# A recurrence whose output gate is summed last, and a quantised feed-forward layer unrolled over the sequences

## The reference, cut to what matters

```python
def step(carry, xg_t):
    h, c = carry
    g = xg_t + h @ W_hh.T
    i, f, gg, o = jnp.split(g, 4, axis=-1)
    c = jax.nn.sigmoid(f) * c + jax.nn.sigmoid(i) * jnp.tanh(gg)
    h = jax.nn.sigmoid(o) * jnp.tanh(c)
    return ((h, c), h)
```

```python
def act_quant_fake(x):
    scale = 127.0 / jnp.clip(jnp.max(jnp.abs(x), axis=-1, keepdims=True), 1e-05)
    return jnp.clip(jnp.round(x * scale), -128.0, 127.0) / scale
# h = layernorm(x) * g1 + b1;  u = gelu(bitlinear(h, w1, b1))
# n = layernorm(u) * g2 + b2;  y = bitlinear(n, w2, b2);  x = layernorm(x + y)
```

## Time and profile before

| what | value |
| --- | --- |
| median of three runs | 2242.31 us (2241.83 to 2244.61) |
| the profiled execution | 2243.14 us, of which the span of instructions is 2241.3 us |
| PE busy | 1638.2 us, 73% of the span |
| DVE busy | 1314.2 us, 59% |
| ACT busy | 912.4 us, 41% |
| POOL busy | 567.8 us, 25% |
| chain that ended last | PE 54%, issue 21%, DVE 8%, ACT 6%, POOL 5% |

### The profile page before, as it was taken

How to read it: one execution, slowest core, us unless ns; L and a number is a source line. 1 busy time by engine, 2 the same in 40 slices (tenths; PEclk the granted TensorE clock), 3 DMA queues, 4 the chain that set the end, 5 groups by cost and what they waited for, 6 DMA issues and landing times.

```text
span 2241.3 us, 44676 instructions
## 1 busy us (share of the span) xinstructions
PE 1638.2 (73%) x14699; PEld 1050.1 (47%) x14699; DVE 1314.2 (59%) x4045; ACT 912.4 (41%) x2545; POOL 567.8 (25%) x937
## 2 busy tenths in 40 slices
PE   4545389667775557898768822159989999996997
PEld 3333255445443335554435511135657777774443
DVE  2333566556666765613756767757756666663776
ACT  2222344456641113443435433223336665653443
POOL 2321422211212223300222233422224334342010
PEclk9999999789986768998989955579989999997999
DMA  5000000000000000000020000000000000000000
GB/s 192 1 1 1 1 1 0 0 1 0 0 0 0 0 0 0 1 1 1 0 82 15 1 1 0 0 1 1 0 1 1 0 0 0 0 1 0 0 0 19
DMA packets 2930, 18.30 MB, mean 8 GB/s; under 512 B 1050, under 2 KB 1178, under 8 KB 1562
## 3 DMA queue, kind: packets, MB, share of 16 engines
q1 hardware_dynamic: 2842, 17.17, 2.0%
HBM read 16.06 MB, written 1.05 MB: 8 GB/s over the span
## 4 chain that ended last, share of the span: by engine, by line
PE 54%; issue 21%; DVE 8%; ACT 6%; POOL 5%; DVEq 3%; POOLq 3%; DMA 0%; ACTq 0%; SPq 0%
PE ps L2876 5%; PE ps L922 3%; PE ps L936 3%; PE ps L2441 3%; PE ps L2451 3%; PE ps L2465 3%; PE ps L2420 3%; PE ps L2427 3%; PE ps L991 2%; PE ps L1502 2%; POOL arena L362 2%; PE ps L2285 2%; PE ps L344 2%; PE ps L901 2%; PE ps L556 1%
## 5 line engine op out<-in xcount | busy, mean ns | idle before, releaser
L362 POOL TENSOR_TENSOR arena<-arena,C 128x1 f32<-128x1 f32 (+1 forms) x240 | 137.5, 575 | 728.1 <-DVE arena L373 415.5
L1081 DVE TENSOR_REDUCE arena<-ps 128x4 f32<-128x512 f32 x256 | 164.0, 685 | 88.3 <-PE ps L932 49.2
L457 POOL TENSOR_TENSOR arena<-arena,C 128x512 f32<-128x512 f32 x96 | 100.0, 1042 | 364.0 <-ACT arena L658 127.2
L2378 POOL TENSOR_TENSOR arena<-arena 128x512 f32<-128x512 f32 x128 | 132.9, 1044 | 233.5 <-DVE arena L2666 232.9
L1049 ACT ACTIVATE arena<-ps 128x512 f32<-128x512 f32 x256 | 132.2, 602 | 89.3 <-PE ps L948 89.3
L1502 PE MATMUL ps<-hid,WA 128*20 128x16 f32 x1024 | 57.8, 197 | 104.9 <-DVE hid L1547 104.9
L2876 PE MATMUL ps<-WA,arena 128*128 128x512 f32 x256 | 133.5, 603 | 0.4 <-ACT arena L2900 0.4
L2575 ACT ACTIVATE arena<-ps,arena 128x256 f32<-128x256 f32 x256 | 120.1, 479 | 11.9 <-issue 8.1
L2584 ACT COPY arena<-ps 128x512 f32<-128x512 f32 x128 | 69.1, 589 | 121.4 <-PE ps L2451 121.4
L2658 DVE TENSOR_REDUCE arena<-ps 128x2 f32<-128x512 f32 x128 | 82.4, 686 | 43.9 <-PE ps L2441 42.5
L1502 PEld LDWEIGHTS ps<-hid,WA 128*20 128x20 f32 x1024 | 44.2, 117 | 127.4 <-DVE hid L1547 127.0
(11 more groups left out here) (435 smaller groups left out, 4190.1 us busy)
## 6 DMA issues: line engine op xcount, KB each, us to landing
WA<-w_late SPq DMA_DIRECT2D x1, 4228.0 KB, 12.9
WA<-w_early SPq DMA_DIRECT2D x1, 1600.0 KB
R<-rows SPq DMA_DIRECT2D x1, 1282.0 KB, 7.0
WB<-w_rest SPq DMA_DIRECT2D x1, 1152.0 KB, 11.3
xT_all<-x_T SPq DMA_DIRECT2D x1, 1024.0 KB, 6.5
x_all<-x_tok SPq DMA_DIRECT2D x1, 1024.0 KB, 13.6
arena<-mask SPq DMA_DIRECT2D x1, 1024.0 KB
ctxT_all<-ctx_T SPq DMA_DIRECT2D x1, 1024.0 KB
```

Source lines behind the costliest of these rows:

```text
L362: nc.gpsimd.tensor_tensor(v_(s, cols, "rstd", 0, n), v_(s, cols, "mv", 1, 2 * n - 1)[:, ::2] if n > 1 else v_(s, cols, "mv", 1, 1), cst("m ...
L1081: red = nc.vector.tensor_reduce(v_(z, ATT, "m", 4 * t, 4), heads(ps[z][t][:, :]), AXX, ALU.max)
L2378: nc.gpsimd.tensor_tensor(p, p, v_(z, LAT, "rec", 4 * u + 2 * x, 2).unsqueeze(2).broadcast_to([128, 2, 256]), ALU.mult).then_inc(l_sub, 1)
```

## The change

In the recurrence the order of the gates is i, f, g, o. The first three lie in the banks of before, the output gate in two banks of its own; PE signals behind the third matmul and again behind the fourth. ACT takes a tanh of 48 columns behind the first signal and one of 16 columns (the output gate) behind the second. The sum of `ff1_down` in `fold_pe` moves to another bank.

The quantised layer loses its loop over pairs and its four `ff_` functions. In their place stands an unrolled pipeline over the sequences with 22 steps (k from -3 to 18), in the form of the other feed-forward layer. In step k DVE works on statistics of x (sequence k+3), h (k+2), u (k+1), statistics of Gelu (k), the normalised n (k-1), the sum with x (k-2) and the output (k-3), and finds the scales of h and n together. ACT takes over the subtraction of the mean of u (with its sign turned), POOL the gain g2 and x plus the offset of the second product; the offset b2 is held in PSUM (`f2_beta`). The four `quantize` steps on a column (maximum with 1e-5, reciprocal, times 127, reciprocal) become a maximum and product, one reciprocal and one product. Counters of other sub-layers that ran through this one (`mid_run`, `tail_run`, `staged_run`) are renumbered.

```diff
-FFN = Columns(("kept", 512), ("x", 128), ("h", 128), ("hT", 128), ("u", FF), ("n", FF), ("nT", FF),
-              ("nbT", FF // 2), ("hbT", 64), ("r", 128), ("stats", 8),
-              ("mv", 4), ("rstd", 2), ("a", 8))
...
+FF2 = Columns(("h", 128), ("hbT", 64), ("u", FF), ("n", FF), ("nbT", FF // 2), ("xb", 128), ("r", 128), ("stats", 18),
+              ("mv", 6), ("rstd", 3), ("peak", 2), ("unit", 2), ("scale", 2), ("back", 2))
+assert QKV_KEPT + FF2.size <= ARENA
...
         gate_banks = [ps[0][1], ps[0][2]]
+        out_banks = [ps[1][2], ps[1][3]]
+        GATE_AT = (0, 1, 3, 2)
...
-            def bank(half):
-                return gate_banks[half][0:LSTM_H, :].rearrange("p (t g b) -> p t g b", t=HALF, g=4)
+            def bank(half, gt):
+                if gt == 3:
+                    return out_banks[half][0:LSTM_H, 0:HALF * BATCH].rearrange("p (t b) -> p t b", t=HALF)
+                return gate_banks[half][0:LSTM_H, 0:3 * HALF * BATCH].rearrange("p (t g b) -> p t g b", t=HALF,
+                                                                                g=3)[:, :, gt, :]
+            def weights(name, gt):
+                return name, 20 * GATE_AT[gt], 20
             def inputs(it, half, gt):
                 xs = xT_all[:, :, bass.ds(it * STEPS + half * HALF, HALF)].rearrange("p b t -> p t b")
-                o = bank(half % 2)[:, :, gt, :]
-                nc.tensor.matmul(o, W_of("ih")[:, 20 * gt:20 * gt + 20], xs, start=gt == 0, stop=False,
+                o = bank(half % 2, gt)
+                nc.tensor.matmul(o, W_of(*weights("ih", gt)), xs, start=gt in (0, 3), stop=False,
                                  skip_group_check=True)
                 for name in ("ih", "hh"):
-                    nc.tensor.matmul(o, bias3[:, BIAS(name, 20 * gt, 20)],
-                                     (half_b if gt < 3 else ones_b)[:, :].rearrange("p (t b) -> p t b", t=HALF),
+                    nc.tensor.matmul(o, bias3[:, BIAS(*weights(name, gt))],
+                                     (ones_b if gt == 2 else half_b)[:, :].rearrange("p (t b) -> p t b", t=HALF),
                                      start=False, stop=False, skip_group_check=True)
...
-                    mm = nc.tensor.matmul(bank(k // HALF)[:, k % HALF, gt, :], W_of("hh")[:, 20 * gt:20 * gt + 20], h,
+                    mm = nc.tensor.matmul(bank(k // HALF, gt)[:, k % HALF, :], W_of(*weights("hh", gt)), h,
                                           start=False, stop=True, skip_group_check=True)
-                mm.then_inc(gates_sum, 1)
+                    if gt >= 2:
+                        mm.then_inc(gates_sum, 1)
...
-                sums = gate_banks[k // HALF][0:LSTM_H, :].rearrange("p (t n) -> p t n", t=HALF)
-                act.wait_ge(gates_sum, g + 1)
-                nc.scalar.activation(gates[:, 0:4, :].rearrange("p g b -> p (g b)"), sums[:, k % HALF, :],
-                                     ACT.Tanh).then_inc(gates_tanh, 1)
+                at = k % HALF
+                act.wait_ge(gates_sum, 2 * g + 1)
+                nc.scalar.activation(gates[:, 0:3, :].rearrange("p g b -> p (g b)"),
+                                     gate_banks[k // HALF][0:LSTM_H, 48 * at:48 * at + 48], ACT.Tanh).then_inc(gates_tanh, 1)
+                act.wait_ge(gates_sum, 2 * g + 2)
+                nc.scalar.activation(gates[:, 4, :], out_banks[k // HALF][0:LSTM_H, 16 * at:16 * at + 16], ACT.Tanh)
                 act.wait_ge(cell_new, g + 1)
-                nc.scalar.activation(tanh_c[:, :], gates[:, 4, :], ACT.Tanh, scale=0.5).then_inc(cell_tanh, 1)
+                nc.scalar.activation(tanh_c[:, :], gates[:, 3, :], ACT.Tanh, scale=0.5).then_inc(cell_tanh, 1)
                 if ABS_FROM <= g < ABS_FROM + 2 * len(TERN):
                     abs_act(act, g - ABS_FROM)
...
-                nc.vector.scalar_tensor_tensor(prod[:, :, :], gates[:, 0:2, :], 1.0, gates[:, 3:5, :], ALU.add, ALU.mult)
+                nc.vector.scalar_tensor_tensor(prod[:, :, :], gates[:, 0:2, :], 1.0, gates[:, 2:4, :], ALU.add, ALU.mult)
                 dve.drain()
-                nc.vector.scalar_tensor_tensor(gates[:, 4, :], prod[:, 1, :], 0.5, prod[:, 0, :],
+                nc.vector.scalar_tensor_tensor(gates[:, 3, :], prod[:, 1, :], 0.5, prod[:, 0, :],
                                                ALU.mult, ALU.add).then_inc(cell_new, 1)
                 dve.wait_ge(cell_tanh, g + 1)
-                nc.vector.scalar_tensor_tensor(hid[g % 2][0:LSTM_H, :], gates[:, 2, :], 1.0, tanh_c[:, :],
+                nc.vector.scalar_tensor_tensor(hid[g % 2][0:LSTM_H, :], gates[:, 4, :], 1.0, tanh_c[:, :],
                                                ALU.add, ALU.mult).then_inc(hid_new, 1)
                 if MEAN_FROM <= g < MEAN_FROM + 5:
...
+        F2_X, F2_H, F2_IN, F2_N, F2_R, F2_OUT = 3, 2, 1, 1, 2, 3
+        f2_beta = ps[1][3]
+        def f2_(n, name, of=0, width=None):
+            c = FF2(name, of, width)
+            return arena[n % 2][:, QKV_KEPT + c.start:QKV_KEPT + c.stop]
+        def f2_steps():
+            return range(-F2_X, BATCH + F2_OUT)
+        def f2_count(k):
+            return k + F2_X + 1
+        def f2_scales(k):
+            return k + F2_H + 1
+        def has(n):
+            return 0 <= n < BATCH
+        def ff2_pool(pool):
+            for k in f2_steps():
+                if k < BATCH + F2_R:
+                    taken = 1 if k < 0 else 2 if k < F2_R else 3
+                    pool.wait_ge(f_var, F1_STEPS + f2_count(k))
+                    nc.gpsimd.tensor_tensor(f2_(k, "rstd", 0, taken), f2_(k, "mv", 1, 2 * taken - 1)[:, ::2],
+                                            cst("minushalf")[:, 0:taken], ALU.pow).then_inc(f_rstd, 1)
+                if has(k):
+                    pool.wait_ge(g_mid, k + 1)
+                    nc.gpsimd.tensor_tensor(f2_(k, "n"), f2_(k, "n"), R[:, ROWS("ff2_g2")], ALU.mult).then_inc(g_gain, 1)
+                    pool.wait_ge(seq_done, ready(S_FF2, k))
+                    nc.gpsimd.tensor_tensor(f2_(k, "xb"), x_all[:, k, :], R[:, ROWS("ff2_down")], ALU.add).then_inc(f_xb, 1)
+        def ff2_pe(pe):
+            def up(n):
+                pe.wait_ge(f_xnT_sb, BATCH + n + 1)
+                nc.tensor.matmul(ps[0][n % 2][:, :], f2_(n, "hbT").bitcast(BF16), tern_up[:, :], start=True,
+                                 stop=True).then_inc(f_up, 1)
+            def turned_n(n):
+                pe.wait_ge(g_n, n + 1)
+                for t in range(4):
+                    mm = nc.tensor.transpose(ps[1][n % 2][:, 128 * t:128 * t + 128], f2_(n, "n", 128 * t, 128), ident)
+                mm.then_inc(f_uT, 1)
+            def down(n):
+                pe.wait_ge(f_uT_sb, BATCH + n + 1)
+                y, nbT = ps[1][2][:, 128 * (n % 2):128 * (n % 2) + 128], f2_(n, "nbT").bitcast(BF16)
+                for t in range(4):
+                    mm = nc.tensor.matmul(y, nbT[:, 128 * t:128 * t + 128], tern_down[:, t, :], start=t == 0, stop=t == 3,
+                                          skip_group_check=True)
+                mm.then_inc(f_y, 1)
+            def turned_h(n):
+                pe.wait_ge(f_xn, BATCH + n + 1)
+                nc.tensor.transpose(ps[0][2][:, 128 * (n % 2):128 * (n % 2) + 128], f2_(n, "h"), ident).then_inc(f_xnT, 1)
+            for k in f2_steps():
+                if has(k + F2_IN):
+                    up(k + F2_IN)
+                if has(k - F2_R):
+                    turned_n(k - F2_R)
+                    down(k - F2_R)
+                if has(k + F2_H):
+                    turned_h(k + F2_H)
+        def ff2_act(act):
+            for k in f2_steps():
+                n = k - 1
+                if has(n):
+                    act.wait_ge(f_var, F1_STEPS + f2_count(n))
+                    nc.scalar.activation(f2_(n, "n"), f2_(n, "u"), ACT.Identity, scale=-1.0,
+                                         bias=f2_(n, "mv", 2, 1)).then_inc(g_mid, 1)
+                n = k - F2_R
+                if has(n):
+                    act.wait_ge(f_uT, BATCH + n + 1)
+                    nc.scalar.activation(f2_(n, "nbT").bitcast(BF16), ps[1][n % 2][:, :], ACT.Identity, scale=-1.0,
+                                         bias=plus_round[:, 0:1]).then_inc(f_uT_sb, 1)
+                n = k + F2_IN
+                if has(n):
+                    act.wait_ge(g_in, n + 1)
+                    nc.scalar.activation(f2_(n, "u"), f2_(n, "u"), ACT.Gelu).then_inc(f_act, 1)
+                n = k + F2_H
+                if has(n):
+                    act.wait_ge(g_scale, f2_scales(k))
+                    nc.scalar.activation(f2_(n, "h"), f2_(n, "h"), ACT.Identity, bias=plus_round[:, 0:1],
+                                         scale=f2_(k, "scale", 0, 1)).then_inc(f_xn, 1)
+                n = k - F2_N
+                if has(n):
+                    act.wait_ge(g_scale, f2_scales(k))
```

(71 more changed lines are left out.)

230 lines of the change are left out of this document (17 added, 213 removed).

## The result

The changed kernel takes **2167.96 us** (median of four runs, 2165.83 to 2171.21), against 2242.31 for the kernel before in the same comparison: a ratio of 0.967, with a 95% interval of 0.966 to 0.9685. One further run of the kernel before took 2755.51 us and is left out of that median. The forecast was 2169, in a range of 2157 to 2184. The profiled execution took 2166.34 us, with a span of 2164.5.

A forecast was written before the change was run, and what follows sets the result against it. Both stretches were taken as chains of hand-overs, not bound by an engine's capacity. 2243.14 - 9.4 (recurrence) - 63.8 (quantised layer) = 2169.9, forecast 2169 us against the median, 8-in-10 range 2157 to 2184.

The forecast's parts named there:

- Part 1: Recurrence, output gate last: ACT is released one gate earlier, 0.075 us a step over 126 steps, 9.4 us.
- The cover for the second tanh: Recurrence: 0.2 us of slack was to hide the output gate's added tanh on ACT.
- Part 2, the step of 6.8: Quantised layer's pipeline over sequences: a full step of 3.99 + 2.8 = 6.8 us against 11.6 a sequence; 63.8 us go.
- The wait for u: Quantised layer: DVE stands ready at 1.42 but unscales u at 1.65, behind PE's up product, a gap of 0.23 us.
- y ends last: Quantised layer: y, the second product, is usable at 3.99 us, 0.37 after DVE is free, and closes the loop.
- the way over POOL: Quantised layer: ACT's u-minus-mean, POOL's gain done by 3.0, n on DVE from about 2.95 to 3.62 us.
- The end of the step: Quantised layer, DVE from the sum's start to the step's last instruction: 1.45 plus largest values and small instructions, together 2.8 us.
- A: Quantised layer's step from the rounding of h to the sum with x, measured at 4.39 to 4.40 us.
- the rule that I cited: Trainium skill: DVE with two SBUF inputs and a reading GpSimd instruction exclude each other; h's second pass waits for POOL's gain.
- The b2 copy: Quantised layer, first filling step: copying offset b2 into PSUM, 0.5 us, bounded by 0.2 and 0.75.
- The clock rival: Quantised layer: PE's clock rises to 2.4 GHz, step 6.3 us, 6.5 us less, 2162 us; chance 20%.
- The rival of port and hand-overs: Quantised layer: two-operand DVE instructions beside POOL cost 1 us a step, step 7.8, 14 us more, 2183 us; chance 17%.

The follow-up runs named there:

- the short PE: Changed kernel with one of n's four transposes and one of its four down matmuls in the quantised layer; 2160.66 us, ratio 0.9633.
- the opened loop: Changed kernel with the sum with x and its statistics moved behind the scale on DVE, y of odd rows in another bank; 2170.5 us, ratio 0.9683.

## Why the prediction was right, by its own steps

- **Sum and state.** 2243.14 − 9.4 − 63.8 = 2169.9 stands against the profiled 2166.34. Of the 3.6 us it is too high, 0.9 are the recurrence, 0.6 the layer, 1.75 the unchanged stretch between them and 0.4 what follows. There the same instructions differ between runs: the first sum of the sub-layer behind the recurrence starts at 284.8 us in the changed kernel and at 282.4 in the variant with the output on POOL, although both have the same code to that point and their first outputs lie 0.2 us apart, at 227.2 and 227.0. That the forecast lies within about 1 us of the median is in part luck: the unchanged stretch alone moves by 5 us from trace to trace.
- **Part 1.** The spacing of passes gave 0.075 a step; the rows after show 0.07 from PE to tanh, and the step is 1.56 rather than 1.58. The missing term is the narrower tanh, 0.20 against 0.21 us. I had given nothing for it, since the 16 columns of `tanh_c` took as long as the 64 of the gates; but those read SBUF, with a scale of 0.5, and these PSUM, without one. The output gate's 16 columns, from PSUM, take 0.16. So I compared unlike forms, and said wrongly that the trace disagrees with the Trainium skill (ScalarE: Activation LUTs, What ACT_TABLE_LOAD costs): its 0.833 ns a column makes an estimated 13 ns of 16 columns, and the trace shows 15 (medians of 214 ns for 64 columns and 199 for 48).
- **The cover for the second tanh** was 0.42, not 0.2 us: I let it start when the first is done, but it starts 0.10 after it.
- **Part 2, the step of 6.8** was 6.69, by partly offsetting terms, and its working doesn't add up. The product, drain and aggregations behind the reciprocal are given as 0.24 and 0.39, which is 0.63, yet the scales are put at -0.52. And with ACT's rounding 0.2 later, at -0.32, the terms 0.55, 0.93 and 0.64 lead to 1.80, not to the 1.65 that is used for u. Measured are 0.55, 0.95 and 0.66, from a rounding at -0.48, and u at 1.68. So the terms were right, the start was 0.16 too late, and the 1.65 was near the truth only because the working departs from its own terms. The wait for u was 0 to 0.2 (0.23 forecast); y was waited for 0.18 (0.37 forecast). That y ends last was right, and the short PE shows it; but it leads the way over POOL by 0.27 us only, and I had taken the two as 0.37 apart on DVE.
- **The end of the step** is 2.29 us from the sum to the rounding. I had 2.8 from the sum to the last instruction, of which 0.52 lie behind the scale; with the hand-over to ACT of 0.2 that makes 2.5, so this half was some 0.2 too long, and A, 4.3 by the same working, 0.1 too short. The mis-sized term is that hand-over: ACT's rounding starts 0.03 us after the reciprocal's end (1349.99 and 0.17, then 1350.19), and 0.20 after its start.
- **DVE and POOL.** h's second pass was stretched to 0.55 by the gain, as by the rule that I cited, and it cost nothing, since n waits for that gain anyway. The b2 copy took 0.69 (0.5 forecast, between bounds of 0.2 and 0.75), once.
- **The layer** took 121.9 us against 122.5. By DVE's last instruction of each step, filling took 18.1 us (17.8 forecast), the twelve full steps 80.0 (81.3), step 14 6.5 (6.6), steps 15 and 16 11.3 together (11.0), step 17 4.4 (4.3).
- **The clock rival** did not occur, and its main support was unsound: the 1.00 of 240 to 270 us. In that very stretch a transpose of 128 columns takes 472 ns, as in the layer at 0.50, and 328 in the other feed-forward layer:

```profile
L1634 PE MATMUL ps<-C,arena x16: 418/472/476, 232.2 to 268.3; 128*128 128x128 f32 x16
...
L2181 PE MATMUL ps<-C,arena x16: 272/328/447, 891.4 to 934.9; 128*128 128x128 f32 x16
```

  The 20% should have been less.
- **The rival of port and hand-overs** (7.8 us a step) did not occur in the changed kernel. Its mechanism, 1 us a step for a two-operand instruction beside POOL, is seen: it is what the opened loop ran into, because there h's first pass comes late enough to meet the gain. In the changed kernel that pass ends 0.17 us before the gain starts.

## What to carry to other kernels

In a pipeline of a few engines, draw the loop that returns to its own start, and split it where two ways meet: an instruction counts only if it stands on the way that arrives last, or between the meeting point and the restart. Here 0.2 us saved on DVE ahead of the meeting point gave nothing, 0.34 behind it gave 0.27, and 0.96 off PE gave 0.27. And compare variants by the stretch that they change: here the unchanged rest scattered by more than most variants won. Before moving an instruction of VectorE that reads two operands from SBUF to a later place, see what GpSimd does there.

## What the runs showed of the hardware

**A granted clock of 1.00 from the start of a trace may be no clock.** Two kernels with the same code in this stretch, the changed one and the one with b2 from SBUF, 12 to 200 us:

```profile
12.00:200.00 188.00, 102.61 (x1447) 69.43 (x1445) 63.25 (x372) 59.70 (x370) 49.84 (x101) 1.00 0.11 42
```

This is the second one's row; the first one's (0.51, PE 102.23 us) stands at the top. The recurrence's passes have a median of 194 ns in both:

```profile
L1504 PE MATMUL ps<-hid,WA x1024: 175/194/233, 12.2 to 214.0; 128*20 128x16 f32 x171
L1504 PE MATMUL ps<-hid,WA x1024: 193/194/231, 12.3 to 214.2; 128*20 128x16 f32 x171
```

The changed kernel alone has a few of 175 ns, ahead of the point where its record falls to 0.50. The second one has none, though its record stands at 1.00 throughout. It looks as if the record shows 1.00 until the first change of level is seen. That is an inference; the durations are what was measured, and they say the same speed.

**The exclusion of VectorE and GpSimd lasts to the end of GpSimd's instruction.** A 128x128 pass with two operands in SBUF, begun 0.07 us after a gain of 1.26 us, took 1.34; begun when the gain had some 0.4 us left, 0.55; with one of the two in PSUM, 0.35 in the same place. A 128x512 pass with both in SBUF, begun when POOL's sum had 0.40 us left, took 0.94 instead of 0.74. In all three cases the pass grew by 0.2 us less than what was left of POOL's instruction (1.19, 0.39 and 0.40 us left, 0.99, 0.20 and 0.20 longer), as if it could do nothing until that instruction was over. The Trainium skill (SBUF — State Buffer, SBUF: two separate sides) calls the shared pair of ports an exclusive lock, held for the whole instruction, not a split of bandwidth. The trace agrees. GpSimd's gain took 1.26 in all of these, whether a pass of VectorE was held back by it or not; what makes it slower than the 1.04 of other products of that shape on POOL is not settled.
